# A perceiver block on one core: another order of work in the shared experts and in the passage to the second cross-attention

## The chip, the cores and the metric

One core of one Trainium2 chip runs the whole program. The metric is the device time of one execution in microseconds (us). The time of the kernel before is the median of three runs.

## The reference

The input is x, 8 sequences of 64 rows with 512 features, a context of 8 x 1601 rows of 512, and a padding mask of the context. Two layers are computed, every step added to x after a layer norm of x:

- Layer 0: cross-attention over the first 64 context rows with a causal mask; self-attention with one weight per head; then a mixture of experts (64 experts of width 352, of which each of the 512 rows takes 8, and shared experts of width 704).
- Layer 1: cross-attention over all 1601 context rows with 16 heads of 32, self-attention, and a matmul with both sides rounded to 8-bit integers.

Two places matter here. The shared experts compute

```python
shared = _mlp(x, Sg, Su, Sd)     # silu(x @ Sg.T) * (x @ Su.T) @ Sd.T
out = (routed + shared).reshape(B, S, H)
```

and the second cross-attention computes, for a layer-normed x as q and the context as kv,

```python
Q = (q @ Wq + bq)...             # 512 rows x 512
KV = (kv @ Wkv + bkv)...         # keys and values of all 8 x 1601 context rows
attn = softmax(where(mask, -inf, Q K^T * scale))
```

## The kernel before

Five engines run their own instruction streams, written out by hand, and meet at semaphores: TensorE (PE, matmuls and transposes), VectorE (DVE), ScalarE (ACT), GpSimd (POOL) and SyncE (SP, which issues most transfers). `wait_ge(s, n)` holds an engine until semaphore s has reached n. PE writes to eight banks of PSUM (`PS[:, bank, :]`); DVE and ACT read them out.

**Shared experts** (`first_pe`, `first_act`, `first_dve`). The 512 rows are four tiles of 128 rows, the width 704 two halves of 352, so there are eight pieces, k = 0 to 7, with tile k // 2 and half k % 2. A piece goes through these steps:

- `shared_in(k)`, PE: four matmuls for the gate and four for the up half (the profile counts two instructions for each fp32 matmul). Line 746.
- `shared_silu(k)`, ACT (line 894), and `shared_mul(k)`, DVE (line 1015): silu of the gate times the up half.
- `shared_out(k)`, PE: three transposes of the product (line 756); then a wait for ACT's copy of them out of PSUM, `shared_ht(k)` (lines 813 and 814); then three down matmuls (line 762), which two pieces of a tile add up in one bank.
- `shared_add(t)`, DVE (line 1019): the sum into x of tile t.

Beside them the routing is worked out: DVE selects the experts, PE sums up ranks (lines 784 and 787, after `sel_ready`), DVE turns the ranks into places, PE transposes the expert column (line 795), and the tables of rows and weights are built in four steps, each of a DVE part (`ab_ready`) and a PE part `table(t)` (line 769). The order on PE was: pieces 0 and 1 in, 0 out, 2 in, 1 out, ranks, 3 in, 2 out, 4 in, expert column, 3 out, 5 in, table 0, 4 out, tables 1 and 2, 5 out, table 3, 6 in, 7 in, 6 out, 7 out.

**The routed loop** follows: tiles of 128 gathered rows, four in flight, some 7.2 us each. `rows_t` on PE (line 2141) transposes gathered rows, `rows_high` on ACT and `rows_low` on DVE (line 2296) split them in two parts, `weights_high` (ACT, line 2011) and `weights_low` (DVE, line 2019) do the same for the weights, `gate_up` on PE (line 2157) multiplies, `hidden_t` transposes (line 2169), `down` (line 2180) ends a tile. Before the loop every engine reads the loop count from memory (`iterations`, line 1144). SP stores x with the shared sums into an accumulator in memory after the fourth `shared_add` (line 2055); the outputs of the routed tiles are added there by POOL's scatters. ACT writes the first routed output only once that store has landed.

**The passage.** After the last routed tile comes layer 1's cross-attention. It needs keys (`k0` to `k3`, blocks of up to 450 context rows, line 1296) and values (`v0` to `v12`, blocks of 128, line 1305) of the first sequence, each of twelve matmuls. Groups write to two banks in turn, so a group waits until the last but one has been read out. A value is read out by DVE (line 1471), a key by ACT (line 1415) and then DVE (line 1478). `PRE[0]` is the order of the first groups. Meanwhile DVE adds the two accumulators (`sums`, after `acc_in`), takes the moments, POOL takes the power, DVE scales (`scaled`, line 1573), PE turns the four tiles (`xt_pe`, line 348), and `q_pe` makes the queries: four pieces of four matmuls of 512 columns (line 369), placed by DVE in `q_dve` (line 379) and split by POOL in `take_q` (lines 1236 to 1241). Then `PRE[1]` follows, with the four score pieces `s0` to `s3` (line 1323, masked by DVE in line 1489). `set_mask` (line 1507) makes the additive mask in four pieces. After the scores ACT takes the exponentials (line 1425), and the units of the attention begin: `T0` is the first group of transposes of probabilities (line 1343).

## Time and profile before

| | us |
|---|---|
| Median of 3 runs | 1679.32 (1677.81 to 1680.35) |
| Profiled execution, its own time | 1682.47 |
| Its span, first to last instruction | 1680.6 |
| PE busy | 1634.1 |
| DVE busy | 966.9 |
| ACT busy | 637.0 |
| POOL busy | 446.1 |

The profile is of one execution, in us from the start of the span. A row of the chain of waits gives start, length, engine and line; the timeline gives an engine's instructions in order, with the idle time ahead in brackets and what ended it. "PEld" is PE's loading of weights, which lies over its matmuls. A queue such as "SPq" is the engine's sequencer. Ends of matmuls are modelled, so two rows of one engine may overlap by some tenths.

### The profile page before, as it was taken

What the parts mean: (1) busy time and instruction counts of PE and PEld (TensorE: products, weight loads), DVE (VectorE), ACT (ScalarE), POOL (GpSimd) and SP (SyncE); (2) the same over time, 40 slices, a digit from 0 to 9 for tenths busy, and PEclk for the clock granted to TensorE, in tenths of its full rate; (3) what the DMA queues carried; (4) which work ended last, traced back from release to release, by engine and by line L of the source; (5) the groups of instructions that cost most, each with busy time, mean ns of one, the idle gap of its engine ahead of it and who ended that gap; (6) DMA issues with size and microseconds to landing.
All of it is one profiled execution on the core that took longest, in us unless ns stands there. A gap on an engine that the chain in (4) does not pass through costs nothing.

```text
span 1680.6 us, 35189 instructions
## 1 busy us (share of the span) xinstructions
PE 1634.1 (97%) x13780; PEld 1351.0 (80%) x13781; DVE 966.9 (58%) x2076; ACT 637.0 (38%) x845; POOL 446.1 (27%) x453
## 2 busy tenths in 40 slices
PE   8999999999999999899999999999999999999897
PEld 5666677788777887778998989989899899898583
DVE  3877566667766666545444445454444544544666
ACT  1232156555655555223334233342242332423112
POOL 3110245555555554210302103021030210400100
PEclk9999999999999999999999999999999999999998
DMA  8003399999999998201102001020020200201200
GB/s 302 13 3 118 136 343 335 344 334 337 336 341 336 340 328 286 92 1 40 41 6 80 6 18 64 7 80 6 1 80 6 67 19 2 79 2 35 98 26 27
DMA packets 68476, 214.92 MB, mean 128 GB/s; under 512 B 13106, under 2 KB 30770, under 8 KB 58496
## 3 DMA queue, kind: packets, MB, share of 16 engines
q1 hardware_dynamic: 38656, 153.03, 25.3%
q10 hardware_dynamic: 15360, 43.26, 7.5%
q0 software_dynamic: 14336, 16.83, 4.8%
q8 instruction: 95, 1.56, 0.4%
q14 instruction: 29, 0.24, 0.0%
HBM read 208.07 MB, written 21.76 MB: 137 GB/s over the span
## 4 chain that ended last, share of the span: by engine, by line
PE 93%; DVE 2%; ACT 1%; DMA 1%; issue 1%; SPq 0%; POOL 0%; DVEq 0%; POOLq 0%; ACTq 0%
PE PS L1305 18%; PE PS L1296 17%; PE PS L2157 14%; PE PS L2180 9%; PE PS L1323 6%; PE PS L1343 6%; PE PS L1362 3%; PE PS L390 3%; PE PS L448 2%; PE PS L746 2%; PE PS L2141 2%; PE PS L411 1%; PE PS L762 1%; PE PS L2169 1%; PE PS L1698 1%
## 5 line engine op out<-in xcount | busy, mean ns | idle before, releaser
L1305 PE MATMUL PS<-S_r 128*128 128x256 f32 x2496 | 329.3, 286 | 1.9 <-DVE kh0l L1478 1.9
L1305 PEld LDWEIGHTS PS<-S_r 128*128 128x128 f32 x2496 | 305.0, 189 | 26.6 <-issue 22.2
L1296 PE MATMUL PS<-S_r 128*128 128x384 f32 (+1 forms) x1536 | 307.3, 349 | 0.0
L2157 PE MATMUL PS<-S_r,R_r 128*128 128x352 f32 x1152 | 298.8, 350 | 1.7 <-DVE R_r L2296 1.7
L1296 PEld LDWEIGHTS PS<-S_r 128*128 128x128 f32 x1536 | 266.2, 188 | 10.7 <-DVE kh0l L1478 2.0
L2157 PEld LDWEIGHTS PS<-S_r,R_r 128*128 128x128 f32 x1152 | 199.6, 189 | 20.5 <-issue 18.6
L1431 ACT COPY S<-PS 128x512 f32<-128x512 f32 (+1 forms) x128 | 64.4, 503 | 276.9 <-PE PS L1343 276.9
L1236 POOL COPY S<-qbd 128x128 f32<-128x128 f32 x32 | 9.4, 293 | 536.6 <-PE PS L1323 525.2
L1489 DVE CUSTOM_DVE_ANT_0 R<-PS,maskadd 128x384 f32<-128x384 f32 (+1 forms) x256 | 136.1, 569 | 17.9 <-PE PS L1323 17.9
L1471 DVE TENSOR_TENSOR R<-PS,vbias 128x256 f32<-128x256 f32 (+1 forms) x208 | 88.1, 424 | 101.3 <-PE PS L1305 96.6
L1219 POOL TENSOR_TENSOR S_r<-S,S_r 128x1536 fp32r<-128x1536 f32 (+2 forms) x31 | 114.0, 3686 | 119.7 <-ACT S_r L1408 119.6
L1425 ACT ACTIVATE R<-R,nmx 128x1601 f32<-128x1601 f32 x64 | 104.0, 1629 | 82.9 <-DVE nmx L1497 82.9
L2180 PE MATMUL PS<-R 128*128 128x512 f32 (+1 forms) x288 | 131.7, 593 | 1.3 <-DVE R L2306 1.3
L1478 DVE SCALAR_TENSOR_TENSOR kh0l<-PS,bias_c,kh0h 128x384 fp32r<-128x384 f32 x64 | 39.5, 618 | 141.6 <-ACT kh0h L1415 141.6
L2104 POOL DMA_INDIRECT moe_acc<-x,scol x64 | 102.4, 1600 | 57.1 <-PE PS L2141 36.1
L2019 DVE TENSOR_TENSOR R_r<-R,S_r 128x1408 fp32r<-128x1408 f32 x64 | 101.1, 1622 | 27.0 <-ACT S_r L2011 27.0
L1343 PE MATMUL PS<-ident,R 128*128 128x128 f32 (+1 forms) x832 | 114.1, 275 | 0.8 <-ACT R L1425 0.8
L1478 DVE SCALAR_TENSOR_TENSOR kh1l<-PS,bias_c,kh1h 128x384 fp32r<-128x384 f32 x64 | 41.7, 651 | 115.1 <-ACT kh1h L1415 115.1
L1523 DVE COPY S<-PS 128x512 f32<-128x512 f32 (+1 forms) x128 | 75.0, 586 | 53.8 <-PE PS L1343 53.4
L1343 PEld LDWEIGHTS PS<-ident,R 128*128 128x128 f32 (+1 forms) x832 | 93.7, 140 | 8.2 <-issue 3.0
L2011 ACT CAST S_r<-R 128x1408 fp32r<-128x1408 f32 x64 | 84.3, 1365 | 41.7 <-PE PS L2157 41.7
L2100 POOL COPY scol<-idx_tab 128x1 int32 (+1 forms) x64 | 62.2, 971 | 111.9 <-ACT x L2238 109.1
(261 smaller groups left out, 2462.6 us busy)
## 6 DMA issues: line engine op xcount, KB each, us to landing
R<-in_w_gu SPq DMA_DIRECT2D x34, 1408.0 KB, 9.7
R<-in_w_dna ACTq DMA_DIRECT2D x45, 512.0 KB, 5.5
qbd<-in_w_gu SPq DMA_DIRECT2D x16, 1408.0 KB, 9.4
S<-in_w_gu SPq DMA_DIRECT2D x16, 1408.0 KB, 9.5
S<-in_ctxT SPq DMA_DIRECT2D x24, 768.0 KB, 4.7
R<-in_w_dnb ACTq DMA_DIRECT2D x45, 192.0 KB, 7.3
xnT<-in_w_dna ACTq DMA_DIRECT2D x15, 512.0 KB, 5.4
S<-in_ctxT SPq DMA_DIRECT2D x8, 898.0 KB, 5.0
```

The costliest lines, as they stand in the source:

```text
L1219: nc.gpsimd.tensor_tensor(lo, raw, hi.bitcast(F32), ALU.subtract).then_inc(s, 1)
L1296: last = nc.tensor.matmul(PS[:, bank, 0:n], w3[0][:, cc, f0:f0 + P], x3[i][:, cc, 0:n], start=(cc == 0 and w3 is wkv_hi and x3 is ctx_hi), ...
L1305: last = nc.tensor.matmul(PS[:, bank, 0:256], x3[need][:, cc, k0:k0 + P], w3[1][:, cc, f0:f0 + 256], start=(cc == 0 and w3 is wkv_hi and x ...
L1323: last = nc.tensor.matmul(PS[:, p, 0:n], q3[r:r + 64, :], k3[r:r + 64, 0:n], start=(q3 is qh and k3 is kh_), stop=(q3 is ql))
L1343: last = nc.tensor.transpose(PS[0:n, 2 + p, i * P:(i + 1) * P], sx[2 * (dc % 2) + p][:, kt * P:kt * P + n], ident[:, :])
L1425: nc.scalar.activation(v, v, ACT.Exp, scale=SC, bias=nmx[:, p:p + 1], accum_out=rsx[:, p:p + 1]).then_inc(px_ready, 1)
L1471: nc.vector.tensor_tensor(vx[hf][0:n, i, :], PS[0:n, bank_of(b, dc, ("v", i)), 0:256], vbias[0:n, hf * 256:hf * 256 + 256], ALU.add).then_ ...
L1489: nc.vector.tensor_tensor_reduce(out=sx[2 * ((dc + 1) % 2) + p][:, k0:k0 + n], in0=PS[:, p, 0:n], in1=maskadd[:, k0:k0 + n], scale=1.0, sc ...
L2019: nc.vector.tensor_tensor(wgu_lo[k][:, c, :, :], wgu[k][:, c, :, :], wgu_hi[k % 2][:, c, :, :].bitcast(F32), ALU.subtract).then_inc(wl_rea ...
L2104: pool.indirect_dma_start(out=acc[k % 2], out_offset=bass.IndirectOffsetOnAxis(ap=scol[:, k:k + 1], axis=0), in_=yrow[k], in_offset=None, ...
L2157: last = nc.tensor.matmul(PS[:, gu, 0:I], x3[:, c, :], w3[:, c, gu, :], start=(c == 0 and x3 is hi[0] and w3 is hi[1]), stop=(c == NC - 1 ...
L2180: last = nc.tensor.matmul(PS[:, 3, :], hT[0:w, j, :], wdn[k][0:w, j, :], start=(j == 0), stop=(j == 2))
```

## The change

It has two parts.

- Shared experts: `shared_in` takes one half (gate, `gu` = 0, or up, `gu` = 1) at a time, and waits only for the reader of its own bank. `shared_out` is cut into `shared_turned` (the transposes) and `shared_out` (the down matmuls), and in PE's order other matmuls stand between the two. The last `shared_out` stands behind the routed loop's first `rows_t`, and DVE's last `shared_add` behind its first `rows_low`.
- Passage: `PRE[0]` begins with v0 in place of k0. The query step becomes one function per piece, and its pieces q0 to q3 stand among the tokens of `PRE[1]`. DVE makes the four mask pieces later, one after the norm's factor and three after the turned rows, and its copy of v10 behind the factor.

```diff
-        def q_pe(pe, w, n, L, bank=4):
+        def query_pe(pe, w, n, L, dc, bank):
 
             pe.wait_ge(xT_ready, NT * (n + 1))
-            for dc in range(NC):
-                for c in range(NC):
...
+            for c in range(NC):
+                last = nc.tensor.matmul(PS[:, bank + dc, :], w[:, c, dc * P:(dc + 1) * P], xnT[:, c, :],
+                                        start=(c == 0), stop=(c == NC - 1))
+            last.then_inc(q_made, 1)
...
-            def shared_in(k):
+            def shared_in(k, gu):
                 t, hf = k // 2, k % 2
                 if k >= 2:
-                    pe.wait_ge(sh_silu, k - 1)
-                    pe.wait_ge(sh_h, k - 1)
...
+                    pe.wait_ge(sh_h if gu else sh_silu, k - 1)
...
+            def shared_turned(k):
+                hf = k % 2
                 pe.wait_ge(sh_h, k + 1)
                 if k >= 1:
                     pe.wait_ge(sh_ht, k)
                 for j, (i0, n) in enumerate(IJ):
                     last = nc.tensor.transpose(PS[0:n, 6, j * P:(j + 1) * P], shid[hf][:, i0:i0 + n], ident[:, :])
                 last.then_inc(sh_t, 1)
+
+            def shared_out(k):
+                t, hf = k // 2, k % 2
                 pe.wait_ge(sh_ht, k + 1)
...
             pe.wait_ge(ld_sh, 96)
-            shared_in(0)
-            shared_in(1)
+            shared_in(0, 0)
+            shared_in(0, 1)
+            shared_in(1, 0)
+            shared_in(1, 1)
+            shared_turned(0)
+            shared_in(2, 0)
             shared_out(0)
-            shared_in(2)
-            shared_out(1)
+            shared_in(2, 1)
+            shared_turned(1)
 
             pe.wait_ge(sel_ready, 1)
...
-            shared_in(3)
+            shared_out(1)
+            shared_in(3, 0)
+            shared_in(3, 1)
+            shared_turned(2)
+            shared_in(4, 0)
             shared_out(2)
-            shared_in(4)
 
             pe.wait_ge(eot_ready, 1)
             nc.tensor.transpose(PS[0:2, 0, 0:P], eot[:, :], ident[:, :]).then_inc(eot_made, 1)
+            shared_in(4, 1)
+            shared_turned(3)
+            shared_in(5, 0)
             shared_out(3)
-            shared_in(5)
+            shared_in(5, 1)
             table(0)
+            shared_turned(4)
+            table(1)
             shared_out(4)
-            table(1)
             table(2)
+            shared_turned(5)
+            table(3)
             shared_out(5)
-            table(3)
-            shared_in(6)
-            shared_in(7)
+            shared_in(6, 0)
+            shared_in(6, 1)
+            shared_in(7, 0)
+            shared_turned(6)
+            shared_in(7, 1)
             shared_out(6)
-            shared_out(7)
+            shared_turned(7)
+
+            return shared_out
...
-            shared_add(3)
...
-        PRE = ["k0 v0 v1 v2 k1 v3 v4 v5 v6 v7 v8 v9 v10 v11", "s0 k2 s1 k3 v12 s2 s3"]
+        PRE = ["v0 k0 v1 v2 k1 v3 v4 v5 v6 v7 v8 v9 v10 v11", "q0 q1 s0 q2 k2 s1 k3 s2 v12 s3 q3"]
...
-            q_pe(pe, wq1, 3, 2, bank=2)
             pe.wait_ge(pads_set, 3)
             for w in PRE[1]:
-                token(-1, 3, w)
+                if w[0] == "q":
+                    query_pe(pe, wq1, 3, 2, w[1], 2)
+                else:
+                    token(-1, 3, w)
...
-            made(("k", 0), ("v", 0), ("v", 1))
+            made(("v", 0))
             first_rest(2, 0)
+            made(("k", 0), ("v", 1))
             first_rest(2, 1)
...
-            made(("v", 4))
-            set_mask(0, 0)
-            set_mask(0, 1)
-            made(("v", 5))
-            set_mask(0, 2)
-            set_mask(0, 3)
-            made(("v", 6))
+            made(("v", 4), ("v", 5), ("v", 6))
...
-            made(("v", 10))
...
+            made(("v", 10))
+            set_mask(0, 0)
...
-            q_dve(dve, 2, 2, bank=2)
+            set_mask(0, 1)
+            set_mask(0, 2)
+            set_mask(0, 3)
...
                 rows_t(0, 0)
+                shared_out(2 * NT - 1)
...
                 rows_low(0, 0)
+                shared_add(NT - 1)
                 weights_low(0, 1)
```

## Rows read from the trace of the kernel before

**Rows 1.** The page, part 1: busy time, share of the span, instructions.
```profile
PE 1634.1 (97%) x13780; PEld 1351.0 (80%) x13781; DVE 966.9 (58%) x2076; ACT 637.0 (38%) x845; POOL 446.1 (27%) x453
```

**Rows 2.** The chain of waits in the shared experts: start us, us, what.
```profile
129.90 9.52 PE PS L746 x32
...
139.42 0.34 PE PS L756 x3
...
208.98 2.86 PE PS L762 x6
...
213.97 3.49 PE PS L2157 x12
...
225.32 2.85 PE PS L2180 x6
...
230.86 1.94 PE PS L2157 x12
...
232.80 2.58 PE PS L2180 x6
```

**Rows 3.** Waits, 125 to 215 us: total us, times, longest.
```profile
PE PS L762 <- ACT R L814: 5.0, 8, 0.6
```

**Rows 4.** Timeline of DVE: start us, us, line, operation [idle before <- releaser].
```profile
144.09 3.68 DVE L1062 TENSOR_REDUCE S<-S 128x256 f32<-128x2048 f32 x1
...
194.80 0.32 DVE L1132 TENSOR_SCALAR idx_tab<-PS,pad_row 128x96 int32<-128x96 f32 x1 [5.04 <-PE PS L769]
```

**Rows 5.** Instructions of line 1144, the value load, on TensorE's weight-load queue.
```profile
L1144 PEldq TENSOR_LOAD <-n_iter x1: 500/500/500, 209.0 to 209.0; - x1
```

**Rows 6.** Busy by stretch of time; the last three are clock, DMA share, GB/s.
```profile
214.00:218.00 4.00, 4.00 (x17) 3.93 (x17) 3.64 (x2) 1.94 (x3) 3.17 (x3) 0.57 0.97 367
...
220.00:227.20 7.20, 6.57 (x37) 5.31 (x36) 6.14 (x8) 5.88 (x6) 0.00 (x0) 1.00 1.00 382
...
457.60:486.40 28.80, 28.80 (x149) 22.95 (x148) 19.96 (x25) 17.39 (x21) 15.56 (x17) 1.00 1.02 336
...
685.00:690.00 5.00, 5.00 (x28) 5.00 (x29) 2.74 (x5) 0.00 (x0) 0.00 (x0) 0.66 0.51 143
```

**Rows 7.** Timeline of SP's queue: start us, us, what was issued.
```profile
212.88 0.47 SPq L2055 DMA_DIRECT2D moe_acc<-x  x1
...
686.91 0.51 SPq L2070 DMA_DIRECT2D R<-moe_acc  x1
```

**Rows 8.** DMA issues: KB each, us from issue to landing.
```profile
moe_acc<-x SPq DMA_DIRECT2D x1, 1024.0 KB, 11.6
...
R<-moe_acc SPq DMA_DIRECT2D x1, 1024.0 KB, 7.9
```

**Rows 9.** Timeline of PE in the passage.
```profile
684.88 4.63 PE L1305 MATMUL PS<-S_r 128*128 128x256 f32 x24 [1.94 <-DVE kh0l L1478]
...
706.89 2.36 PE L348 MATMUL PS<-ident,S 128*128 128x128 f32 x16 [2.18 <-DVE S L1573]
...
710.13 13.97 PE L369 MATMUL PS<-xnT,R 128*128 128x512 f32 x32 [0.88 <-DVE xnT L358]
...
733.94 0.47 PE L1323 MATMUL PS<-kh1h,qb0h 64*128 64x450 f32 x2 [1.33 <-DVE mx L1489]
...
739.80 0.66 PE L1343 MATMUL PS<-ident,R 128*128 128x128 f32 x4 [0.82 <-ACT R L1425]
```

**Rows 10.** Timelines of DVE and of POOL in the passage.
```profile
696.61 0.79 DVE L1507 TENSOR_SCALAR maskadd<-mask 128x384 bf16<-128x384 uint8 x2
...
697.59 0.42 DVE L1471 TENSOR_TENSOR R<-PS,vbias 128x256 f32<-128x256 f32 x1 [0.19 <-PE PS L1305]
...
704.21 0.42 DVE L1471 TENSOR_TENSOR R<-PS,vbias 128x256 f32<-128x256 f32 x1
...
713.84 1.53 DVE L379 TENSOR_SCALAR qbd<-PS,bias_c,halfmask 128x512 f32<-128x512 f32 x2 [3.86 <-PE PS L369]
...
716.41 0.46 POOL L1241 TENSOR_TENSOR qb0l<-S,qb0h 128x128 fp32r<-128x128 f32 x1
```

More of the change, by code:

```diff
@@ L362, in xt_copy, with query_dve @@
                 turned_copy(eng, copy, n, t, t)
-        def q_pe(pe, w, n, L, bank=4):
+        def query_pe(pe, w, n, L, dc, bank):
             pe.wait_ge(xT_ready, NT * (n + 1))
-            for dc in range(NC):
-                for c in range(NC):
-                    last = nc.tensor.matmul(PS[:, bank + dc, :], w[:, c, dc * P:(dc + 1) * P], xnT[:, c, :],
-                                            start=(c == 0), stop=(c == NC - 1))
-                last.then_inc(q_made, 1)
-        def q_dve(dve, L, bias, bank=4):
-            for dc in range(NC):
-                dve.wait_ge(q_made, NC * L + dc + 1)
-                src = PS[:, bank + dc, :].rearrange("p (b q) -> p b q", b=B)
-                for h in range(2):
-                    last = nc.vector.tensor_scalar(qbd[:, dc, :, h * S1:(h + 1) * S1], src, bias_c[:, bias, dc:dc + 1],
-                                                   halfmask[:, h:h + 1], ALU.add, ALU.mult)
-                last.then_inc(q_ready, 1)
+            for c in range(NC):
+                last = nc.tensor.matmul(PS[:, bank + dc, :], w[:, c, dc * P:(dc + 1) * P], xnT[:, c, :],
+                                        start=(c == 0), stop=(c == NC - 1))
+            last.then_inc(q_made, 1)
+        def query_dve(dve, L, bias, dc, bank):
+            dve.wait_ge(q_made, NC * L + dc + 1)
+            src = PS[:, bank + dc, :].rearrange("p (b q) -> p b q", b=B)
+            for h in range(2):
+                last = nc.vector.tensor_scalar(qbd[:, dc, :, h * S1:(h + 1) * S1], src, bias_c[:, bias, dc:dc + 1],
+                                               halfmask[:, h:h + 1], ALU.add, ALU.mult)
+            last.then_inc(q_ready, 1)
         SC_B, PT_B, ZT_B, Q_B, T_B, O_B = 0, 2, 3, 5, 6, 7
@@ L737, in first_pe @@
             logits(3)
-            def shared_in(k):
+            def shared_in(k, gu):
                 t, hf = k // 2, k % 2
                 if k >= 2:
-                    pe.wait_ge(sh_silu, k - 1)
-                    pe.wait_ge(sh_h, k - 1)
-                for gu in range(2):
-                    for c in range(NC):
-                        last = nc.tensor.matmul(PS[:, 2 + 2 * hf + gu, 0:I], xnT[:, c, t * P:(t + 1) * P],
-                                                wgu[2 + hf][:, c, gu, :], start=(c == 0), stop=(c == NC - 1))
-                    last.then_inc(sh_u if gu else sh_g, 1)
-            def shared_out(k):
-                t, hf = k // 2, k % 2
+                    pe.wait_ge(sh_h if gu else sh_silu, k - 1)
+                for c in range(NC):
+                    last = nc.tensor.matmul(PS[:, 2 + 2 * hf + gu, 0:I], xnT[:, c, t * P:(t + 1) * P],
+                                            wgu[2 + hf][:, c, gu, :], start=(c == 0), stop=(c == NC - 1))
+                last.then_inc(sh_u if gu else sh_g, 1)
+            def shared_turned(k):
+                hf = k % 2
                 pe.wait_ge(sh_h, k + 1)
@@ L1137, in first_dve @@
             shared_add(2)
-            shared_add(3)
+            return shared_add
         def iterations(eng):
@@ L1162, in perceiver @@
                "v0 v1 k0 v2 T0 k1 s0 v3 v4 T1 k2 s1 v5 v6 v7 P0 P1 T2 z0 k3 s2 v8 v9 v10 T3 s3 v11 v12 P2 P3"]
-        PRE = ["k0 v0 v1 v2 k1 v3 v4 v5 v6 v7 v8 v9 v10 v11", "s0 k2 s1 k3 v12 s2 s3"]
+        PRE = ["v0 k0 v1 v2 k1 v3 v4 v5 v6 v7 v8 v9 v10 v11", "q0 q1 s0 q2 k2 s1 k3 s2 v12 s3 q3"]
         words = lambda text: [(w[0], int(w[1:])) for w in text.split()]
         SEQ, PRE = [words(unit) for unit in SEQ], [words(text) for text in PRE]
-        PRE_MADE = [w for part in PRE for w in part if w[0] != "s"]
+        PRE_MADE = [w for part in PRE for w in part if w[0] in "kv"]
         MADE = [[w for w in unit if w[0] in "kv"] for unit in SEQ]
```

9 lines of the change are left out of this document (6 added, 3 removed).

## The prediction

> **What bounds the kernel now.** I read the page first: TensorE (PE) is busy for 97% of the span [rows 1], so only two things can shorten the time: pauses of PE, and stretches in which it runs slowly. The chain of waits says where they lie. In the shared experts, which run from 129.90 to 211.84 us, every piece shows one pattern: three transposes (0.34 us), a pause, and six down matmuls in 2.86 us, as the last piece shows from 208.98 us [rows 2]. The table of waits counts the pause: 8 times, 5.0 us, so 0.62 us each, ended each time by ScalarE's (ACT's) copy of the transposed hidden rows [rows 3]. The same six matmuls in the routed loop, where something runs directly ahead of them, take 2.58 us on the chain against 2.85 us behind a pause (the ones at 232.80 and at 225.32 us) [rows 2]: a restart costs 0.27 us more.
>
> Two stretches run at the lower clock. In 214 to 218 us the mean granted clock is 0.57, in 685 to 690 us it is 0.66, so part of each was at 1.2 GHz [rows 6]. Before the first PE had paused from the last down (end 208.98 + 2.86 = 211.84) to 213.97, and its first twelve gate matmuls then took 3.49 us, against 1.94 us later [rows 2]. The second follows a pause of 1.94 us, and 24 value matmuls took 4.63 us [rows 9].
>
> In the passage the timelines of PE and of VectorE (DVE) belong together. PE makes values until DVE has added, normed and scaled the rows, pauses 2.18 us, turns them, makes all four query pieces in 13.97 us from 710.13 us, and pauses 1.33 us before the last score and 0.82 us before the first transposes of probabilities at 739.80 us [rows 9].
>
> **Part A, the shared experts.** The same matmuls run in the order written by hand. Before seven of the eight down groups there is now a gate half, an up half (piece 7's), the rank group or a table group between the transposes and the down matmuls. One gate half is a quarter of 9.52 us, 2.38 us [rows 2], well over ACT's 0.62 us, and none of the fills needs the piece it covers. Removed: 8 x (0.62 + 0.27) = 7.12 us.
>
> New waits. PE reaches the rank matmuls at 139.42 + 0.34 + 2.38 + 2.58 + 2.38 + 0.34 = 147.44 us; DVE's selection ends at 144.09 + 3.68 = 147.77 us [rows 2, 4], so 0.33 + 0.27 = 0.60 us are lost there. Each up half still waits for the product two pieces back, which is long made. The expert column is transposed before the up half of piece 4, so DVE gets it sooner too and its table steps keep ahead of PE. The last table group then has five down groups' stalls less ahead of it (4.45 us), and the sixth down group with its pause (3.5 us) behind it: less the 0.6 us, it ends 7.3 us earlier. The index table, written from 194.80 us on [rows 4], comes at about 187.5 us and the gathers leave as much earlier. They were not awaited before, and are not now.
>
> The last down group goes behind the first routed rows' transposes. These cover ACT's copy only partly (0.44 us of 0.62 us), so 0.17 + 0.27 = 0.44 us stay. In exchange the pause from 211.84 to 213.97 us disappears, all but the transposes that lay in it, because the last down (2.58 us) now covers ACT's and DVE's work on those rows: 1.7 us. Three engines read the loop count there. On PE the load takes 0.50 us and started at 209.0 us, while the last down ran from 208.98 us [rows 2, 5]: the queue had run ahead. It now comes behind the transposes of piece 7, and the 2.58 us of piece 6's down lie over it, so I cost it at 0; uncovered it costs about 0.85 us (0.50 us and its two followers), the upper bound. DVE's count load now falls between the third and fourth sum, ahead of what it needs, 0.
>
> The first routed gate then starts 7.12 - 0.60 - 0.44 + 1.7 = 7.8 us earlier, at about 206.2 us. If there is no pause ahead of it, its clock stays at 2.4 GHz and the 3.49 us become 1.94 us: 1.55 us. That is 9.35 us.
>
> Not all of it need last. The store of the rows into the accumulator waits for the fourth shared sum, which now waits on DVE behind the first routed rows; queued behind it on SP are the loop's weight loads. It was issued at 212.88 us and took 11.6 us [rows 7, 8], landing at 224.5 us; the first routed output at 225.32 + 2.85 = 228.2 us [rows 2] didn't wait. Now it can leave at about 207.1 us and lands at 218.7 us, and the output is ready at 218.2 us: the slack of 3.7 us is gone. ACT waits 0.5 us there, with its next silu, the loads of down weights and the first scatter and gather of the loop behind it; more if the loads, packed closer, slow each other. I take 0.55 us off for that: part A gives 8.8 us, between 5.8 us (all that the store moves) and 9.8 us.
>
> **Part B, the passage.** Before, PE made k0, then v0, and v1 waited for k0's low half, which DVE ends at 684.83 us because ACT must first convert two blocks of context. That moment stays. But with v0 first, v1 doesn't need k0, so it fills the pause, and v2 starts at 684.88 us. One value group (half of 24 matmuls at full rate, 1.5 us) and the low clock (4.63 us less 3.0 us, 1.6 us) are won: v6 ends 3.1 us earlier, and DVE's copy of it, at 697.59 us before [rows 10], comes at about 694.4 us. DVE is ready for that because the mask pieces (four, of which the last two took 0.79 us [rows 10]) are no longer ahead. The sums also need both accumulators, of which the last was issued at 686.91 us and took 7.9 us [rows 7, 8]: 694.8 us. So they start 3.1 us earlier, held by that landing, with no slack. From there DVE is the bound up to the norm's factor; v10's copy (0.34 us on the chain, starting at 704.21 us [rows 10]) moves behind it. The queries start 3.4 us earlier, at about 706.7 us.
>
> Behind that, the sum of PE's work is unchanged and only its pauses go. A query piece is 13.97 / 4 = 3.49 us [rows 9]. s0 comes after q1: until then DVE must place q0 and POOL split it. Before, DVE began that at 713.84 us and POOL was done at 716.41 + 0.46 = 716.87 us [rows 10]: 3.0 us, under q1's 3.49 us, so 0. q2 covers DVE's first masking, v12 that of s2 (I keep 0.3 us), and q3 with v0 and k0 covers the maximum and the exponentials that were awaited. Removed: 1.33 + 0.82 + 2 x 0.27 = 2.7 us, less 0.3 us: 2.4 us. The other mask pieces fall into DVE's wait for q0. Part B gives 3.4 + 2.4 = 5.8 us, between 2.7 us (sums held by the accumulators as late as before) and 6.5 us.
>
> **Sum.** 8.8 + 5.8 = 14.6 us. The profiled execution's own time is 1682.47 us for a span of 1680.6 us, so the changed one should show a span near 1666 us; it lies 3.15 us above the median of 1679.32 us, which is execution to execution. From the median: 1664.7 us.
>
> **Rivals.**
> - The clock (15%). The falls at 214 and 685 us stood behind pauses of about 2 us, but PE also paused 2.18 us ahead of the turns at 706.89 us [rows 9], and the sixteen turns and the queries behind it ran at full rate (13.97 / 32 = 0.44 us each, the rate of 2.58 / 6 = 0.43 us). So a pause does not decide it alone: one of the two falls may stay, or a new one come in the shortened pause before the queries. Each costs about 1.6 us; with two, 1667.9 us. The Trainium skill, "TensorE: Matmul & The Clock Gate", Part 1, says that the gate's watch runs free of the kernel's start; by that rule, the same pauses can meet a fall in one version and not in the other, as this trace's three pauses do.
> - The transfers hold the first routed tiles (13%). In the loop the DMA share is 1.02 at 336 GB/s, in 220 to 227 us 1.00 at 382 GB/s [rows 6]. So there is only a tenth of room to work off what is packed closer at the start, and part A shrinks to the 5.8 us that the store moves: 1667.7 us. The Trainium skill, "DMA: Bandwidth & Descriptors", section "Issuing engines are not separate DMA queues", says that transfers of SP, ACT and POOL interleave on the same engines: what SP brings forward slows ACT's and POOL's.
> - The accumulators land later than the sums want them (8%): part B's first half gives 0.3 us, 2.7 us in all: 1667.8 us.
> - The new order does not fill (5%): if PE's queue stops at other signals, for instance for products that DVE makes late between its table steps, part A gives only the 3.25 us at its end and the total is 9 us: 1670.3 us.
> - Slower (4%). The loop becomes bound by transfers for good. It has 63 intervals in the 451 us up to the last tile; the same bytes at a rate below 336 x (1 - 14.6 / 451) = 325 GB/s eat all, and at 315 GB/s the time is 336 / 315 x 451 - 451 - 14.6 = +15.5 us, 1694.8 us. For it speaks the share of 1.02; against it, that the same engines moved 382 GB/s with full queues.
>
> **Numbers.** My case has 55%, with 1662.5 to 1667 us of its own. Two of the rivals for less gain end near 1668 us, so 1661.5 to 1670 us holds eight in ten. A measurement of this kernel tells 0.2%, 3.4 us: all cases but the last lie beyond it. Faster 0.94, same 0.02, slower 0.04.
>
> **What would show it.** In the profile after: no pause by ACT's copy ahead of the down matmuls, but one of 0.3 us at the rank matmuls; the index table near 187.5 us; the first routed gate near 206 us at full clock and the first routed down near 216 us; then PE without a pause. In the passage (all 8.8 us earlier as well) two pauses less, 3.4 us gained at the queries, and the first transposes of probabilities 14.6 us before 739.80 us, near 725.2 us. A wait of the routed rows on a gather, a low clock in 205 to 215 or 690 to 705 us, or a DVE wait for the accumulators would make it wrong in turn.

## The result and the profile after

The changed kernel takes 1670.71 us (median of 5 executions, 1668.19 to 1674.52) against 1679.48 us (5 executions beside it): ratio 0.9946, interval 0.9935 to 0.9957. That is 8.8 us less, where 14.6 us were forecast, and 0.7 us above the range. Later executions of the same two kernels on three chips gave 0.9934, 0.9941 and 0.9932, between the medians 10.9 to 12.5 us. All 22 executions of the changed kernel have a median of 1669.5 us, the 60 of the kernel before that ran in these comparisons 1680.1 us: 10.6 us less, the best figure here. The sign was right, the size was too high by 4 to 6 us.

The profiled execution took 1670.71 us, for a span of 1668.8 us. Part 1 of its page answers to [rows 1]:

```profile
PE 1629.5 (98%) x13780; PEld 1348.8 (81%) x13781; DVE 966.7 (58%) x2076; ACT 637.1 (38%) x845; POOL 446.5 (27%) x453
```

PE is busy for 4.6 us less although it does the same work. So the 11.8 us that the span lost are not pauses alone; the clock has a part in it. Up to the last 30 us the profile before has four stretches of some 3.4 us at half clock (at 214.5, 685.5, 1559.3 and 1590.0 us), the one after has two (at 237.0 and 697.8 us).

**Shared experts.** The table of PE's waits from 125 to 215 us, against [rows 3]:

```profile
PE PS L2177 <- DVE R_r L2317: 0.8, 1, 0.8
...
PE PS L787 <- DVE S L1078: 0.4, 1, 0.4
PE PS L761 <- ACT R L830: 0.2, 1, 0.2
```

The eight pauses by ACT's copy have become one of 0.2 us, and the rank matmuls (L787) wait 0.4 us for DVE. One wait was not foreseen: 0.8 us of the first routed tiles for DVE's low half of the rows (L2317). The index table on DVE's timeline, against [rows 4]:

```profile
186.72 0.32 DVE L1148 TENSOR_SCALAR idx_tab<-PS,pad_row 128x96 int32<-128x96 f32 x1 [3.02 <-PE PS L768]
```

PE's timeline at the start of the loop:

```profile
204.86 0.72 PE L2177 MATMUL PS<-S_r,R_r 128*128 128x352 f32 x1
...
210.48 2.19 PE L2177 MATMUL PS<-S_r,R_r 128*128 128x352 f32 x12 [0.76 <-DVE R_r L2317]
...
215.20 2.74 PE L2200 MATMUL PS<-R 128*128 128x512 f32 x6
...
236.58 0.80 PE L2161 MATMUL PS<-ident,S 128*128 128x128 f32 x4 [1.95 <-DMA S<-moe_rows,gcol]
```

The first routed gate starts at 204.86 us instead of 213.97 us and the first routed down at 215.20 us instead of 225.32 us [rows 2]: 10.1 us earlier, of which 0.9 us was already there ahead of the shared experts. Then the sixth tile's rows are awaited for 1.95 us, and the clock falls. The windows (busy time by engine, then clock, DMA share, GB/s), against [rows 6], show the same 0.57 there and at the turning of the rows in the passage:

```profile
236.50:240.50 4.00, 3.92 (x16) 3.92 (x17) 0.69 (x1) 0.59 (x1) 1.72 (x3) 0.57 0.99 346
697.50:701.50 4.00, 3.63 (x16) 3.23 (x16) 2.67 (x7) 1.17 (x2) 0.00 (x0) 0.57 0.00 0
```

From the first to the fourth routed down it takes 25.36 us, against 21.73 us before. Where that comes from is seen on three queues. SP's, with the landing from the view of DMA issues, against [rows 7, 8]:

```profile
206.52 0.51 SPq L2075 DMA_DIRECT2D moe_acc<-x  x1
...
681.10 0.51 SPq L2090 DMA_DIRECT2D R<-moe_acc  x1
```
```profile
moe_acc<-x SPq DMA_DIRECT2D x1, 1024.0 KB, 13.7
```

ACT's and POOL's timelines:

```profile
215.77 2.64 ACT L2031 CAST S_r<-R 128x1408 fp32r<-128x1408 f32 x2 [1.71 <-DMA R<-in_w_gu]
220.29 0.69 ACT L2259 ACTIVATE x<-PS,w_tab 128x512 f32<-128x512 f32 x1 [1.89 <-DMA moe_acc<-x]
```
```profile
221.12 0.18 POOL L2120 COPY scol<-idx_tab 128x1 int32<-128x1 int32 x1 [10.37 <-ACT x L2259]
...
224.89 1.10 POOL L2109 DMA_INDIRECT S<-moe_rows,gcol  x1 [0.86 <-POOL gcol L2105]
```

The store leaves at 206.52 us (forecast 207.1) and takes 13.7 us instead of 11.6 us, so it lands at 220.2 us (forecast 218.7). ACT waits 1.89 us for it, POOL's first scatter waits for ACT, and the gather behind that scatter leaves at 224.89 us and is awaited until 236.58 us.

**Passage.** PE's timeline, against [rows 9]:

```profile
681.35 8.85 PE L1322 MATMUL PS<-S_r 128*128 128x256 f32 x72
690.83 4.90 PE L1322 MATMUL PS<-S_r 128*128 128x256 f32 x36 [0.63 <-DVE R L1490]
697.65 3.63 PE L348 MATMUL PS<-ident,S 128*128 128x128 f32 x16 [1.92 <-DVE S L1592]
702.16 7.11 PE L368 MATMUL PS<-xnT,R 128*128 128x512 f32 x16 [0.88 <-DVE xnT L358]
...
721.55 0.48 PE L1340 MATMUL PS<-kh1h,qb0h 64*128 64x450 f32 x2 [0.16 <-DVE mx L1508]
...
729.45 1.04 PE L1360 MATMUL PS<-ident,R 128*128 128x128 f32 x8
...
732.50 0.44 PE L1340 MATMUL PS<-kh0h,qb1h 64*128 64x384 f32 x2
```

The pauses of 1.94, 1.33 and 0.82 us are gone. A pause of 0.63 us is new, that ahead of the turns is 1.92 us (2.18 before), and the sixteen turns take 3.63 us at the lower clock, against 2.36 us. The last row is the first score matmul of the next unit, 30.34 us behind the first query matmul. In the profile before it stands 32.35 us behind it:

```profile
742.48 0.44 PE L1323 MATMUL PS<-kh0h,qb1h 64*128 64x384 f32 x2
```

DVE's timeline shows what holds the sums:

```profile
688.94 1.29 DVE L1586 TENSOR_TENSOR x<-x,R 128x512 f32<-128x512 f32 x2 [1.11 <-DMA R<-moe_acc]
```

### The profile page after: what moved, and what is told of

Its sections match the earlier page's. It is cut to its first block, busy times and chain, and to the rows that moved or that the text cites. A ratio compares the mean times of both kernels' runs of the same rounds, so it can differ in the third digit from the quotient of the medians.

```text
span 1668.8 us, 35182 instructions
## 1 busy us (share of the span) xinstructions
PE 1629.5 (98%) x13780; PEld 1348.8 (81%) x13781; DVE 966.7 (58%) x2076; ACT 637.1 (38%) x845; POOL 446.5 (27%) x453
## 4 chain that ended last, share of the span: by engine, by line
PE 90%; DMA 4%; DVE 2%; issue 2%; ACT 1%; SPq 1%; POOL 0%; POOLq 0%; ACTq 0%; DVEq 0%
PE PS L1322 18%; PE PS L1313 17%; PE PS L2177 13%; PE PS L2200 9%; PE PS L1360 6%; PE PS L1340 6%; PE PS L1379 3%; PE PS L388 3%; PE PS L446 2%; DMA S<-moe_rows,gcol 2%; PE PS L742 2%; PE PS L2161 1%; PE PS L409 1%; PE PS L761 1%; PE PS L2189 1%
```

## The experiments

Two questions: which part of 14.6 us did not come, and why. The theories for the loop's start were: theory 1, the late store (ACT and POOL wait for its landing); theory 2, packed transfers (everything that the change brings forward meets in full queues, and gathers and weights land late whatever the store does); theory 3, chance of one execution; and theory 4, POOL's order (a gather leaves only behind the output ahead of it). Theories 5 and 6 came up later, and are told with their runs.

**e1_a_only.** Part A alone: of the diff only `shared_in`, `shared_turned`, `shared_out` and their order, the `shared_add` and the last down behind `rows_t(0, 0)`; the passage as before.

```diff
 PRE = ["k0 v0 v1 v2 k1 v3 v4 v5 v6 v7 v8 v9 v10 v11", "s0 k2 s1 k3 v12 s2 s3"]
...
                 rows_t(0, 0)
+                shared_out(2 * NT - 1)
```

> The kernel before with part A alone (shared experts split, last down group behind the first routed rows). In the profile of the whole change the first routed down starts 9.2 us earlier than before, counted from the first shared matmul, and the fourth routed down only 5.6 us earlier: 3.6 us are lost in a pause for a gather and the low clock behind it. Theory 1 (the store of the rows into the accumulator lands late, ACT's first routed output waits, the gather goes out late) and theory 2 (the transfers packed closer make the gather late whatever the store does) both expect the same loss here, since part B plays no role there: 5.6 us at the end of the routed loop, total 5 to 6.5 us under the kernel before. Theory 3 (the pause is chance of one execution) expects 8 to 9.5 us.

Measured: 1673.15 us, ratio 0.9962 [0.9952, 0.9973], so 6.4 us (4.5 to 8.1; 7.4 us between the medians). Its PE timeline has the pause of the sixth tile too (1.87 us at 236.92 us).

**e2_b_only.** Part B alone: the new `PRE`, the query pieces and the masks; the shared experts as before. Of its difference to the kernel before:

```diff
-        PRE = ["k0 v0 v1 v2 k1 v3 v4 v5 v6 v7 v8 v9 v10 v11", "s0 k2 s1 k3 v12 s2 s3"]
+        PRE = ["v0 k0 v1 v2 k1 v3 v4 v5 v6 v7 v8 v9 v10 v11", "q0 q1 s0 q2 k2 s1 k3 s2 v12 s3 q3"]
```

> The kernel before with part B alone (v0 first, masks later, query pieces among the scores). If the parts add up, this gives the rest: 3.5 us if the low clock stays behind the pause before the turned rows, 5 us if it does not fall there. In the profile: the sums held by the landing of the accumulators, the queries 1.3 us (with the low clock) to 2.8 us (without) closer to the last routed down than before, and 2.2 us more from there to the first transposes of probabilities.

Measured: 1676.61 us, ratio 0.9983 [0.9971, 0.9994], so 2.9 us (1.0 to 4.9; 3.9 us between the medians). The parts sum to 6.4 + 2.9 = 9.3 us, where the whole gave 11.1 us (8.2 to 13.9) on the same chip: they add up within the intervals, and both are smaller than forecast. The turns wait 1.92 us here too, at 703.24 us, with the lower clock behind it. At 214 us, where this kernel still has before's pause of 1.7 us, the clock did not fall.

**e3_both.** The changed kernel again, beside these.

> The changed kernel again, beside its parts. 7.5 to 10 us under the kernel before. Theories 1 and 2: ACT's first routed output waits for the store again, a pause of 1 to 2.5 us before the turned rows of the sixth routed tile, and PE at 1.2 GHz behind it in some executions. Theory 3: no pause here.

Measured: 1669.01 us, ratio 0.9934 [0.9917, 0.9951]. Its PE timeline at the sixth tile and in the passage:

```profile
237.62 0.90 PE L2161 MATMUL PS<-ident,S 128*128 128x128 f32 x4 [2.29 <-DMA S<-moe_rows,gcol]
...
698.82 2.36 PE L348 MATMUL PS<-ident,S 128*128 128x128 f32 x16 [1.92 <-DVE S L1592]
```

The pause at the sixth tile is there again; the lower clock at the turns is not, behind the very same pause of 1.92 us.

**e4_split.** The store in four pieces, each sent when its rows are summed, so that only 256 KB are late.

```diff
...
+                def store(t):
+                    sp.wait_ge(sh_y, t + 1)
+                    sp.dma_start(acc[0][t * P:(t + 1) * P, :], x[:, t, :]).then_inc(acc_out, 16)
+
+                load(0, 0, lambda: store(0))
+                load(0, 1, lambda: store(1))
+                load(0, 2, lambda: store(2))
+                load(0, 3)
+                store(3)
...
```

> The changed kernel with the store of x into the accumulator cut into four, one per tile of 128 rows, each issued as soon as its shared sum is made: three leave while the queues are nearly empty, the last is a quarter of the size. Theory 1: the last quarter lands before the first routed output is ready, ACT does not wait, the gather goes out 2 us earlier, no pause; 3 to 3.6 us faster than the changed kernel. Theory 2: the store does land earlier but the gather is still slow (its 11.6 us to landing against 8.7 us in the loop), a pause of 1 us or more stays; 0 to 1.5 us faster.

Measured: 1670.96 us, ratio 0.9945 [0.9926, 0.9965]: no gain. In the view of DMA issues the last quarter took almost as long as the whole, and the pause on PE's timeline grew:

```profile
moe_acc<-x SPq DMA_DIRECT2D x1, 256.0 KB, 12.5
```
```profile
238.18 1.11 PE L2166 MATMUL PS<-ident,S 128*128 128x128 f32 x4 [3.06 <-DMA S<-moe_rows,gcol]
```

A landing that takes 12.5 us for 256 KB, and 13.4 us for 1024 KB in e3_both, says more of what runs in the queues beside it than of its own size. ACT no longer waited for the store. But it waited 2.34 us for gate and up weights instead, so the gather left at 225.09 us, as in e3_both (225.22 us), and landed later still. The late store alone is not the cause.

**e5_nostore.** No store at the loop's start; zeros are written early in its place, so x with the shared experts' sum is left out of the output.

```diff
...
+            for t in range(NT):
+                sp.dma_start(acc[0][t * P:(t + 1) * P, :], zero512).then_inc(acc_out, 16)
...
-                    if k == NBUF - 1:
-                        sp.wait_ge(sh_y, NT)
-                        sp.dma_start(acc[0][0:T, :].rearrange("(t p) d -> p t d", p=P), x[:, :, :]).then_inc(acc_out, 16)
...
```

> The changed kernel without the store of x into the accumulator: zeros are written there instead, with the other zeros, 80 us earlier (so attention and shared sums are missing from what layer 1 gets). It takes 1 MB out of the stretch in which the routed loop begins, and with it ACT's wait for the landing. Theory 2 (the transfers packed at the start make a gather late) expects the pause before the sixth routed tile to shrink from 1.9 to 2.3 us to under 0.5 us, with no low clock behind it: 3 to 3.6 us faster than the changed kernel. If the 1 MB doesn't matter and only POOL's order does, the gather leaves 1 us earlier at most and a pause of 1 us or more stays: 0 to 1.5 us faster.

Measured: 1668.76 us, ratio 0.9943 [0.993, 0.9956]. In the trace the pause is gone (first to fourth down 21.63 us; the gather leaves at 223.63 us), but another gather is awaited for 1.15 us at 502.25 us. In the time nothing shows.

**e6_gather_first.** In the loop's first round POOL sends each gather ahead of the scatter before it.

```diff
-                for k in range(NBUF):
-                    gather(1, k)
+                gather(1, 0)
+                for k in range(NBUF - 1):
+                    gather(1, k + 1)
                     scatter(0, k)
+                scatter(0, NBUF - 1)
```

> The changed kernel with POOL's order changed in the first round only: the gather of routed tile 6 stands ahead of the first scatter instead of behind it (and the next two likewise), so it doesn't wait for the first routed output. Theory 4 (the transfers are slow, 11.6 to 13 us for a gather, but what makes PE pause is that this gather leaves only behind the first output; it could leave 10 us earlier) expects the gather on its way by 212 us, no pause before tile 6, full clock, and 3 to 3.6 us over the changed kernel. Theory 2 (the engines are full, and what is moved forward slows something else) expects another pause of 1 us or more in 225 to 250 us, on weights or on another gather, and 0 to 1.5 us.

Measured: 1670.02 us, ratio 0.995 [0.9937, 0.9963]. No pause at the sixth tile, but one of 1.27 us at 257.64 us, where the first round ends and the old order begins: the late gather had moved.

**e7_tail_undone.** The last shared down and sum back ahead of the first routed rows.

```diff
             shared_turned(7)
-
-            return shared_out
+            shared_out(7)
...
-                shared_out(2 * NT - 1)
```

> The changed kernel with the last shared down group and the last shared sum back ahead of the first routed rows, as before the change. By the prediction's own sum this costs 2.1 us of pause and 1.5 us of low clock at the first routed gate. By theory 2 and 4 the loss at tile 6 is paid only by a kernel that starts the loop early: the pause for the gather shrinks to 0 to 0.5 us and the total is within 1.5 us of the changed kernel.

Measured: 1670.58 us, ratio 0.9949 [0.9937, 0.9962]. In the trace the first routed down comes 2.2 us later than with the tail moved, and no gather is late at the loop's start (three are later on, by 0.3 to 0.6 us). Up to the last down it takes 541.5 us from the last router matmuls; four profiles of the changed kernel take 538.5 to 542.6 us, 540.9 us on the mean. So on the mean most of what the moved tail gives at the loop's start is given back in the loop, as far as one profile tells.

**e8_keep_busy.** Twelve spare matmuls in the pause ahead of the turns; their result is not used.

```diff
+            for i in range(12):
+                nc.tensor.matmul(PS[:, 5, 0:256], ctx_hi[0][:, 0, 0:P], wkv_hi[1][:, 0, 0:256], start=True, stop=True)
             xt_pe(pe, 3)
```

> The changed kernel with twelve spare matmuls (128 x 256, into a PSUM bank that nobody reads) between the last value group and the turning of the rows in the passage, where PE pauses 1.9 us. They take 1.5 us at full rate, less than the pause. If the low clock seen in 698 to 701 us in the profile of the change comes from that pause, it does not appear here: turns to queries 3.3 us instead of 4.6 us, and 0 to 1.3 us faster in the median (in the second profile of the changed kernel it did not fall there either, so it is not in every execution). If the low clock doesn't hang on the pause, it appears as often as before.

Measured: 1669.39 us, ratio 0.9946 [0.9933, 0.9959]. The pause there is 0.50 us and the clock stays full at the turns; in the time nothing shows. And at the sixth tile, where this kernel is the changed one, the gather was late by only 0.16 us:

```profile
234.57 0.66 PE L2163 MATMUL PS<-ident,S 128*128 128x128 f32 x4 [0.16 <-DMA S<-moe_rows,gcol]
```

So the long pause is no fixed price of the change. The profiles of the changed kernel, of e1_a_only and of e3_both were alike on it (1.95, 1.87 and 2.29 us); this one is not. From here on the theories were: theory 5, that the half-clock stretches counted in the prediction were chance, and theory 6, that the gather lands at the edge of being late.

**e9_before_again.** The kernel before, for a second profile, with no edit.

> The kernel before, unchanged, for another profile. Theory 5 (two of the terms of the predicted sum, 1.55 us at the first routed gate and 1.5 us at the passage's values, were half-clock stretches that fell there by chance in the one execution that was profiled, and not something that the change takes away): in this profile at least one of the half-clock stretches at 214.5 and 685.5 us is missing, the span is about 1.6 us shorter for each that is missing anywhere, and the two pauses that are thought to bring them, 1.7 us before the first routed gate and 1.94 us before the passage's second values, are there as before. Rival (the stretches belong to the pauses): both stretches stand at 214 and 685 us again.

Measured: its own time is 1675.5 us, its span 1673.6 us, 7 us under the profile that the prediction used, and a little under the fastest of the 60 other executions (1675.8 us). A typical execution lies between these two profiles. PE's timeline, against [rows 9] and the chain's 213.97 us in [rows 2]:

```profile
213.33 0.43 PE L2157 MATMUL PS<-S_r,R_r 128*128 128x352 f32 x1 [1.71 <-DVE R_r L2296]
...
681.80 3.11 PE L1305 MATMUL PS<-S_r 128*128 128x256 f32 x24 [1.88 <-DVE kh0l L1478]
...
702.26 2.36 PE L348 MATMUL PS<-ident,S 128*128 128x128 f32 x16 [2.19 <-DVE S L1573]
```

The windows of the same two places:

```profile
213.00:218.00 5.00, 4.67 (x29) 4.38 (x30) 4.49 (x4) 2.87 (x5) 4.17 (x3) 1.00 1.03 369
681.00:687.00 6.00, 5.20 (x38) 5.20 (x39) 3.44 (x6) 0.00 (x0) 0.10 (x1) 1.00 0.42 133
```

Both pauses are there, and the clock is full behind both: 24 values in 3.11 us, not 4.63 us, and twelve gate matmuls on the chain in 2.20 us, not 3.49 us. The two stretches were in the sum with 3.15 us, more than half of the 5.8 us by which it missed the first measurement.

**e10_after_again.** The changed kernel a third time, with no edit.

> The changed kernel once more, for another profile and more timed executions: ratio 0.993 to 0.996. Theory 6 (the loop's first gathers land at the edge of being late, so that the pause before the sixth routed tile's turning comes in some executions, with 3.6 us from the first to the fourth down, and not in others): from the first to the fourth routed down the trace shows either about 21.7 us with no pause over 0.5 us, or 25 to 26 us with a pause of about 2 us and a half-clock stretch behind it, and nothing between. Rival (it belongs to the change always, and the trace of the one execution without it was odd): 25 to 26 us.

Measured: 1669.26 us, ratio 0.9941 [0.9927, 0.9954]. First to fourth down 21.62 us, no pause at the sixth tile, and one of 0.18 us on a gather at 256.97 us. The windows show the turns and the first queries at the lower clock for 6.6 us of these 8, about twice as long as in the profile after:

```profile
694.00:702.00 8.00, 6.50 (x20) 3.92 (x21) 4.55 (x10) 1.17 (x2) 0.00 (x0) 0.59 0.07 23
```

**e11_gather_ahead.** POOL sends each gather one tile ahead of the scatter through the whole loop, and the spare matmuls of e8_keep_busy are in.

```diff
-                for k in range(NBUF):
-                    gather(1, k)
+                gather(1, 0)
+                for k in range(NBUF - 1):
+                    gather(1, k + 1)
                     scatter(0, k)
                 with pool.Fori(2, n) as r:
                     for k in range(NBUF):
                         gather(r, k)
-                        scatter(r - 1, k)
+                        scatter(*(tile_before(r - 1, k)))
+                scatter(n - 2, NBUF - 1)
```

> POOL gathers one tile further ahead of its scatters through the whole loop, and 12 spare matmuls lie in the pause before the turning of the rows. Theory 6 and the edge of the gather: no pause before a routed tile's turning in the first 60 us of the loop, first to fourth down 21.6 to 21.8 us; against the changed kernel up to 1 us better on average, so 1667.5 to 1670 us and a ratio of 0.9925 to 0.9955. Rival (what the late gather costs comes back elsewhere in the loop, which the transfers of weights pace): the same time as the changed kernel, with another pause later in the loop. The spare matmuls are expected to make no difference over 0.5 us.

Measured: 1666.60 us, ratio 0.9919 [0.9907, 0.9932]: 13.5 us under the kernel before, 2.7 us under the changed kernel on the same chip. The table of PE's waits from 205 to 660 us no longer has a wait for a gather:

```profile
PE PS L2181 <- DVE R_r L2321: 0.7, 1, 0.7
```

The same table of the changed kernel has two, at 236.58 and 505.41 us:

```profile
PE PS L2161 <- DMA S<-moe_rows,gcol: 2.5, 2, 1.9
```

**e12_second_sum_early.** The second accumulator's load replaced by one of the kernel's input, issued early.

```diff
+                sp.dma_start(x_odd, a["x"]).then_inc(acc_in, 16)
                 for i in range(2):
                     sp.wait_ge(y_added[i], 16 * (NBUF // 2) * n)
-                for i, dst in enumerate((x[:, :, :], x_odd)):
-                    sp.dma_start(dst, acc[i][0:T, :].rearrange("(t p) d -> p t d", p=P)).then_inc(acc_in, 16)
+                sp.dma_start(x[:, :, :], acc[0][0:T, :].rearrange("(t p) d -> p t d", p=P)).then_inc(acc_in, 16)
```

> The load of the second accumulator is replaced by a load of as many bytes of the kernel's own input, issued 8 us earlier, right behind that of the query weights, so the sum leaves out the odd tiles' products; the load of the first accumulator alone still waits for the last scatter. Theory (in the passage the sums are held by the landing of the accumulators, which came 0.8 us later after the last down than the prediction had it): VectorE's wait of 1.1 us for the accumulators goes, the sums start 18.0 to 18.2 us behind the last down instead of 19.0, the queries 30.0 to 30.3 us behind it instead of 30.85, and the time is 0.5 to 1.1 us less than that of the changed kernel: 1668 to 1670 us. Rival (VectorE's own queue holds the chain): the sums start earlier and the queries do not.

Measured: 1668.84 us, ratio 0.9936 [0.9924, 0.9949], no different from the changed kernel. DVE's wait did not go:

```profile
684.68 1.30 DVE L1586 TENSOR_TENSOR x<-x,R 128x512 f32<-128x512 f32 x2 [1.31 <-DMA x<-moe_acc]
```

The one load left took 5.3 us instead of 7.8 us, but SP could issue it only at 679.35 us, 13.9 us behind the last down, where the changed kernel's are issued 10.6 to 11.2 us behind it: the scatters that it waits for ended later. The sums started 19.2 us behind the last down, against 19.0 us in the changed kernel. So neither theory was tested; that the early load itself delayed the scatters is likely, not shown.

**e13_gather_ahead_only.** As e11_gather_ahead, without the spare matmuls.

> The changed kernel with POOL's gathers one tile further ahead, without the spare matmuls. If the gathers' order is the whole of the gain seen before: 1666 to 1668 us, 2 to 3 us under the changed kernel beside it, no pause of PE on a gather anywhere in the loop. If the spare matmuls have a part in it: 1668 to 1669.5 us.

Measured: 1666.95 us, ratio 0.9926 [0.9913, 0.994]. It comes to the same time without the spare matmuls, so the order of the gathers does it. Against e15_after_third on the same chip it gains only 0.8 us, and each of these medians has five or six executions; what the order is worth in the changed kernel is some 1 to 3 us.

**e14_before_gather_ahead.** The same order of gathers in the kernel before.

> The kernel before with the same order of gathers. Theory 6 (late gathers at the start of the loop are a loss that the change brought): here they take away at most the pause near 512 us, 0 to 1.2 us, ratio 0.9990 to 1.0000. Rival (earlier gathers are worth the same in both kernels, and the change lost nothing by them): 2.5 to 3 us less, ratio 0.998 to 0.9985.

Measured: 1678.29 us, ratio 0.9987 [0.9978, 0.9996]: 1.9 us less. That lies between the two expectations, and it is as much as the changed kernel gains by it (2.7 and 0.8 us). With the gathers ahead on both sides the change is worth 1678.29 - 1666.95 = 11.3 us.

**e15_after_third.** The changed kernel a fourth time, with no edit.

> The changed kernel beside the other two: 1668.5 to 1671 us, ratio 0.993 to 0.996. Theory 5 (where a half-clock stretch falls is chance) expects any number from none to two stretches between 200 and 720 us; theory 6 expects from the first to the fourth routed down either 21.6 to 22.1 us or 25 to 26 us.

Measured: 1667.75 us, ratio 0.9932 [0.9918, 0.9945]. First to fourth down 23.46 us: a pause of 1.61 us at 236.32 us, and full clock behind it. Theory 6 had nothing between 22.1 and 25 us, which falls: the gather is late by any amount from 0 to 3 us, and the half clock may follow or not.

## Why the prediction missed

The table has the times between marks on PE's timeline, each the difference of the starts of two rows. The first mark is the last router matmuls ahead of the shared experts, "outputs" the first matmul that waits for the second layer's output weights, some 1550 us in. The last row counts half-clock stretches of 3.4 us between 200 and 720 us; one of 6.8 us counts as two.

| us | before | e9, before | after | e3 | e10 | e15 |
|---|---|---|---|---|---|---|
| to the first routed down | 96.53 | 94.98 | 87.29 | 87.25 | 87.26 | 87.28 |
| to the fourth | 21.73 | 21.74 | 25.36 | 25.71 | 21.62 | 23.46 |
| to the last | 429.55 | 428.66 | 429.35 | 429.62 | 429.64 | 429.64 |
| to the queries | 33.53 | 31.96 | 32.25 | 30.83 | 31.63 | 31.66 |
| to the outputs | 849.34 | 850.13 | 847.32 | 847.51 | 848.49 | 849.02 |
| to the end | 121.13 | 117.98 | 119.32 | 119.63 | 119.74 | 119.65 |
| stretches | 2 | 0 | 2 | 1 | 2 | 2 |

**The step that failed is the clock's two terms**, 1.55 us ("its clock stays at 2.4 GHz") and 1.6 us ("the low clock"), 3.15 us in all. They were read off one execution, and counted as removed because the pauses ahead of them would go. e9_before_again has the pauses and not the stretches. Of the five profiles that keep the pause of 1.7 us ahead of the first routed gate (before, e2, e7, e9, e14) only the one that the prediction used has the stretch behind it; of the four with the pause of 1.9 us in the values (before, e1, e9, e14) two have it. And new ones came: all four profiles of the changed kernel have stretches elsewhere. A stretch costs 1.3 to 1.6 us where it falls (turns to queries 4.51 us in the changed kernel, 3.24 us in e3_both).

The mean granted clock, which is on record for every execution, says the same of all of them: 0.9950 on the mean of the 60 executions of the kernel before, 0.9954 of the 22 of the changed one, 0.993 in the profile used. That is 16.9 us at half clock against 15.3 us, worth 0.8 us in time, give or take 1.2 us, where 3.15 us were forecast. The profile used was also 3.15 us above the median of its kernel, which the prediction put down to the execution and took off both sides; that was a warning. The rival named "the clock" described what happened, with 15% and as an alternative to the others, where it held in every profile of the change and together with them. The Trainium skill, "TensorE: Matmul & The Clock Gate", Part 1, says that the gate's watch runs free of the kernel's start; the stretches that come and go behind one unchanged pause of 1.9 us agree.

**Part A without the clock was right up to the first routed down.** 9.35 us less 1.55 us is 7.8 us up to the first routed down; the table gives 94.98 - 87.27 = 7.7 us. Inside it, the eight pauses went, the rank wait was 0.43 us for a forecast 0.33 us, the last down's 0.19 us for 0.17 us, and the value load cost nothing. The index table came 7.2 us earlier by the mark (7.3). The gate was 0.4 us better than forecast (76.95 us behind the mark, 85.18 us before), and a new wait of 0.76 us for DVE's low half took that back: DVE's last shared sum (0.69 us) and a split of weights (3.75 us) run directly ahead of it.

**The term of the store, 0.55 us, was mis-sized.** The store left as worked out, but landed 1.5 us later, and ACT waited 1.89 us for it, not 0.5 us. What reached PE was the gather behind it, which the prediction expected not to be awaited: from the first to the fourth down 0 to 4 us more in the four profiles, 2.3 us on the mean, of which 1.5 us are pause and the rest half-clock stretches behind it. The seven profiles in which the start of the loop is that of the change show what the pause goes with:

| us | e10 | e12 | e8 | e15 | e3 | after | e1 |
|---|---|---|---|---|---|---|---|
| the store, to its landing | 12.3 | 12.6 | 13.1 | 13.3 | 13.4 | 13.7 | 14.5 |
| ACT waits for it | 0.77 | 0.99 | 1.52 | 1.73 | 1.84 | 1.89 | 3.14 |
| the gather leaves, behind the first down | 8.45 | 8.48 | 9.00 | 9.22 | 9.32 | 9.69 | 10.62 |
| PE waits for the gather at the sixth tile | 0 | 0 | 0.16 | 1.61 | 2.29 | 1.95 | 1.87 |

A gather that left up to 9.0 us behind the first down was hardly awaited, one that left 9.2 us behind it or later was, by 1.6 us or more; in the profile before it left 7.69 us behind. So theories 1 and 3 belong together: the change took the slack, and what is left over varies with the store's landing from one execution to the next. e4_split shows that it is only one of the landings that can hold ACT (9.40 us there, and a pause of 3.06 us). e5_nostore, e6_gather_first and e7_tail_undone each show no late gather at the sixth tile, but so do e8_keep_busy (0.16 us) and e10_after_again without an edit there, so none of them alone proves its cause. What stands is e11_gather_ahead and e13_gather_ahead_only: with gathers one tile further ahead, e13 goes from the last router matmuls to the last down in 537.15 us, the kernel before with the same order (e14_before_gather_ahead) in 544.95 us, so part A keeps 7.8 us through the whole loop. The rival of the transfers had the right place (the first routed tiles) and a fair price, 3 us, but not the reason: e13 moves the same bytes and waits for no gather, so it was the order on POOL and the time to landing, not room on the DMA engines. Seven profiles that agree are no experiment, and why the store lands after 12.3 us in one execution and after 13.7 us in the next stays open.

**Part B without the clock was 1.1 us too high.** The sums were to start 3.1 us earlier, "held by that landing". They did start with the landing, but it came 19.0 us behind the last down, not 18.2 us: the accumulators' loads took 7.8 us as forecast, and were issued 10.8 us behind the last down where the profile used had 9.9 us (10.5 us in e9_before_again). Compared with e9_before_again, whose sums start 19.76 us behind the last down, the order of v0 and the masks gives only 0.7 us, and v10's copy 0.34 us: 31.96 - 30.83 = 1.1 us at the queries, for 3.4 us forecast with the clock in it. The rival "the accumulators land later" (8%) was thus partly true too. Behind the queries 2.0 us came for 2.4 us: to the first score matmul of the next unit it is 32.3 to 32.4 us in before, e1, e9 and e14, and 30.3 to 30.4 us in after, e2, e3, e5, e6 and e13. That is the length of the pauses that went, 1.33 + 0.82 - 0.16 us; the two restarts at 0.27 us do not show. Sum of part B: 3.1 us for 5.8 us; e2_b_only measured 2.9 us.

**The sum again.** 14.6 us, less 3.15 us for stretches, less 1.1 us in part B, less 0.9 us (1.5 - 0.55) for late gathers, is 9.4 us, and 0.8 us more if the clock gave that. Measured are 8.8 us at first, 10.6 us over all executions, and 10.9 to 12.5 us in the other three comparisons; medians of 5 or 6 executions vary by 1 to 2 us with where stretches and late gathers fall, so the sum fits no better than that. Neither the order that "doesn't fill" nor the loop bound by transfers came true: from the fourth to the last down the loop takes the same within 1 us.

## What to carry to other kernels

A slow stretch of the clock is a term of a sum only if it stands there in more than one execution: take a second profile, or compare the profiled execution's own time and mean granted clock with those of the others, before counting it. When work is moved ahead, ask for each queue not only when its next transfer can leave but how much stands ahead of it in full DMA engines; a small transfer there took almost as long as a big one. Gathers of a software pipeline should be issued ahead of the scatters that wait for compute, by one tile more than a quiet trace seems to need.

## What the runs showed of the hardware

- Between 200 and 720 us the half-clock stretches seen here lasted 3.4 or 6.8 us, and they came behind pauses of 1.7 to 3.1 us in some executions and not in others; behind the pause of 2.2 us ahead of the turns in before, e1, e9 and e14 none came. At the turns, with a pause of 1.92 us ahead of them, the clock fell in after, e2, e4, e7, e10, e12 and e15, and not in e3, e5, e6 and e13; with the pause cut to 0.50 us (e8, e11) it did not fall. Two profiles don't prove the latter, and no gain in the time shows.
- 256 KB took 12.5 us (e4_split) and 1024 KB 13.7 us (after) to land from the same point of SP's queue, while the DMA share was 1.02 and 1.03 and a gather of POOL's ran beside them.
- A gather of 128 rows that was awaited in this stretch landed 10.6 to 13.1 us after it was issued (e8, e1, after, e15, e3, e4).
